# Gated cross-attention with a ternary feed-forward: 16-bit projections, halves made in place, another order on every engine

## The chip, the cores and the metric

The kernel runs on one NeuronCore of a Trainium2 chip. The metric is device time of one launch, in microseconds; of three runs of the kernel before the median is 1662.82 us (1661.55 to 1668.23). Engine names as the profile has them: PE (TensorE matmuls), PEld (its weight loads), DVE (VectorE), ACT (ScalarE), POOL (GpSimd), SP (SyncE, which here only starts transfers).

## The reference

All arithmetic is float32. `x` is 128 x 128 x 256 (batch, position, channel), `ctx` is 128 x 128 x 192, 16 heads of 16 channels.

```python
def attn(x, ctx, mask):                       # x is normalised first
    q = split_heads(x @ Wq); k = split_heads(ctx @ Wk); v = split_heads(ctx @ Wv)
    s = where(mask, q @ k.T * 16 ** -0.5, -max)
    return merge_heads(softmax(s) @ v) @ Wo
x = x + tanh(g_xattn) * attn(layernorm(x), ctx, mask)
h = gelu(layernorm(x) @ ternary(W1).T + b1)
x = x + tanh(g_ffn) * (h @ ternary(W2).T + b2)
```

`ternary` rounds a weight, divided by the mean of the weights' absolute values, to -1, 0 or 1.

## The kernel before, in words

The whole of `x` stays in SBUF (`xres`). Stage one is the attention. It goes through 64 groups of two batches; stage two, the feed-forward, goes through 32 steps of four batches and is hardly touched by the change. Each engine runs its own instruction list, written out by hand in Python; engines meet at semaphores only, and every engine runs its list strictly in order. In the loop a group `g` works on the scores of its own two batches and, at the same time, prepares the next three groups (`g1`, `g2`, `g3`).

A group has eight slots on PE, one per unit of four heads (`scores(pe, g, b, u, ...)`). A slot holds four exact score matmuls and four rough ones (`rough_head`), which give DVE the row maxima of a unit further on (`take_max`); then the weighing of an earlier unit (`weigh`), and one or two pieces of the preparation. These are: `transpose_x` and `transpose_ctx`, `project_q`, `project_k`, `project_v` in float32, `transpose_max` (the row maxima of a batch, rounded and split into two float16 parts by `round_max` and `low_max`), `transpose_attn` and `project_out`. All transposes and the output projection write the same PSUM bank, `tr_bank`; the q, k and v projections write `pj_bank`. Each PE function is given in `tr` who must have emptied `tr_bank` before it starts.

Numbers that must be exact in 16-bit matmuls are split into a high and a low half. For q and k, ACT copies PSUM to the float16 high half (`high_q`, `high_k`) and DVE subtracts (`low_q`, `low_k`). For the probabilities ACT writes the exponentials in float32 (`exponentials`); their upper 16 bits, read as bfloat16, are the high half, and POOL makes the low half in a tile of its own (`low_prob`, `probl`).

The halves of q and k reach the layout that the scores need by DMA (`move_heads`, eight transfers per batch, started by SP). The row maxima go the same way: PE transposes them, ACT copies them to `smaxT` (`copy_maxT`), and SP starts the transfer (`move_max`).

The layer norm before the attention is 14 small steps per group on DVE (`ln_part`, L672 to L697), spread one by one between the larger DVE instructions (`norm(i)`); three Newton steps give the root. ACT applies it (`apply_x`).

The functions that the change touches, with their lines, are these.

## Time and profile before

| | |
|---|---|
| median of three runs | 1662.82 us |
| profiled execution, its own time | 1664.17 us |
| span of its trace | 1662.4 us |
| mean granted TensorE clock | 0.984 |
| PE busy | 1508.0 us (91%) |
| DVE busy | 1489.1 us (90%) |
| ACT busy | 939.8 us (57%) |
| POOL busy | 668.8 us (40%) |

The span runs from the first to the last instruction; 1.8 us of the profiled execution lie around it. Busy times are of each engine alone and overlap each other. A matmul's duration in the trace includes the time until its last result is out, so that consecutive matmuls overlap: the distance between two starts says what one costs, the duration says when a reader can begin. The same holds in a smaller way for DVE and ACT. The attention stage takes about the first 1130 us, the feed-forward the rest.

### The profile page before, as it was taken

How to read it: one execution, taken by the hardware profiler on the slowest of the kernel's cores; microseconds unless marked ns; L12 is line 12 of the kernel's file. 1: busy time of each engine (PE TensorE's matmuls, PEld its weight loads, DVE VectorE, ACT ScalarE, POOL GpSimd, SP SyncE). 2: the span in 40 equal slices, each digit the busy share in tenths (PEclk: the TensorE clock that was granted, in tenths of full speed). 3: DMA queues.
4: the chain of work that ended last, by engine and by line, in shares of the span. 5: the costliest groups of instructions: out<-in, count | busy, mean ns of one | idle time of the engine just before them, and what ended most of it. 6: DMA issues, size and time to landing. Idle time of an engine off the chain costs nothing.

```text
span 1662.4 us, 48262 instructions
## 1 busy us (share of the span) xinstructions
PE 1508.0 (91%) x14501; PEld 1007.7 (61%) x14501; DVE 1489.1 (90%) x4379; ACT 939.8 (57%) x1799; POOL 668.8 (40%) x813
## 2 busy tenths in 40 slices
PE   3899999999999999999999999987999999999998
PEld 2566666666666666666666666655666666666665
DVE  7799999999999999999999999987888888888886
ACT  2456666665656666565656566654555555555554
POOL 5354555455555545554555545552111111111111
PEclk9899999999999999999999999996999999999999
DMA  2333333333333333333333333321010110101101
GB/s 78 92 99 85 96 84 88 93 86 97 84 96 83 97 84 94 86 87 95 86 97 83 98 83 95 81 49 55 26 38 25 38 38 25 38 25 38 38 25 51
DMA packets 207471, 117.93 MB, mean 71 GB/s; under 512 B 24912, under 2 KB 207184, under 8 KB 207440
## 3 DMA queue, kind: packets, MB, share of 16 engines
q1 hardware_dynamic: 207440, 117.54, 26.2%
q8 instruction: 17, 0.28, 0.1%
q14 instruction: 14, 0.11, 0.0%
HBM read 32.53 MB, written 16.78 MB: 30 GB/s over the span
## 4 chain that ended last, share of the span: by engine, by line
PE 55%; DVE 26%; issue 13%; ACT 3%; DVEq 2%; ACTq 0%; DMA 0%
PE bank L1069 12%; PE bank L312 9%; PE bank L1098 5%; PE bank L1099 5%; DVE smax L751 5%; PE bank L336 5%; PE bank L319 4%; PE bank L303 4%; DVE rstd L691 3%; DVE xres L796 3%; DVE k L721 3%; PE bank L392 2%; DVE rstd L693 2%; DVE y L1056 2%; DVE rstd L684 2%
## 5 line engine op out<-in xcount | busy, mean ns | idle before, releaser
L924 POOL TENSOR_TENSOR probl<-prob 128x512 f16<-128x512 f32 x512 | 529.2, 1042 | 531.2 <-ACT prob L602 530.3
L602 ACT ACTIVATE prob<-bank,masks 128x512 f32<-128x512 f32 x512 | 345.4, 688 | 138.9 <-PE bank L371 138.9
L751 DVE TENSOR_REDUCE smax<-bank 128x4 f32<-128x512 f32 x512 | 348.2, 681 | 13.5 <-PE bank L336 9.7
L1085 DVE TENSOR_TENSOR hidl<-hid 128x512 f16<-128x512 f32 x256 | 226.0, 883 | 80.5 <-ACT hid L1080 79.7
L1080 ACT ACTIVATE hid<-bank,b_sb 128x512 f32<-128x512 f32 x256 | 176.1, 688 | 211.3 <-PE bank L1069 205.3
L1069 PE MATMUL bank<-y,w1T 128*128 128x512 f16 x1024 | 264.6, 381 | 29.2 <-DVE y L1056 28.0
L1163 POOL TENSOR_TENSOR xres<-xres,b2g 128x1024 f32 (+1 forms) x32 | 75.7, 2366 | 431.4 <-ACT yln L1033 413.5
L1098 PE MATMUL bank<-w2T,hid 128*128 128x256 f16 x1024 | 237.4, 273 | 0.6 <-ACT w2T L1013 0.6
L1099 PE MATMUL bank<-w2T,hidl 128*128 128x256 f16 x1024 | 237.4, 273 | 0.0
L336 PE MATMUL bank<-k_rows,q_rows 64*128 64x128 f16 x2048 | 226.8, 220 | 5.6 <-DMA q_rows<-smaxT 3.4
L371 PE MATMUL bank<-q_rows,k_rows 64*128 64x128 f16 x2048 | 201.7, 219 | 0.8 <-DMA q_rows<-smaxT 0.8
L392 PE MATMUL bank<-v,prob 128*128 128x48 f16 x2048 | 179.4, 187 | 0.7 <-POOL probl L924 0.7
L336 PEld LDWEIGHTS bank<-k_rows,q_rows 64*128 64x128 f16 x2048 | 121.7, 94 | 84.8 <-issue 63.2
L393 PE MATMUL bank<-v,probl 128*128 128x48 f16 x2048 | 172.3, 184 | 0.0
L312 PE MATMUL bank<-ctxT,wk_sb 128*128 128x256 f32 (+1 forms) x512 | 165.2, 430 | 0.9 <-ACT ctxT L553 0.8
L319 PE MATMUL bank<-wv_sb,ctxT 128*128 128x256 f32 (+1 forms) x512 | 163.4, 418 | 0.9 <-DVE k L721 0.9
L1069 PEld LDWEIGHTS bank<-y,w1T 128*128 128x128 f16 x1024 | 97.9, 98 | 104.2 <-issue 35.1
L392 PEld LDWEIGHTS bank<-v,prob 128*128 128x128 bf16 x2048 | 125.4, 97 | 55.0 <-issue 1.8
L303 PE MATMUL bank<-xlnT,wq_sb 128*128 128x256 f32 x512 | 142.2, 402 | 9.7 <-DVE v L742 8.9
L371 PEld LDWEIGHTS bank<-q_rows,k_rows 64*128 64x128 f16 x2048 | 129.3, 95 | 30.0 <-DMA q_rows<-smaxT 1.2
L411 PE MATMUL bank<-wo_sb,attnT 128*128 128x256 f32 x512 | 145.4, 407 | 1.1 <-ACT attnT L610 1.1
L393 PEld LDWEIGHTS bank<-v,probl 128*128 128x128 f16 x2048 | 130.0, 97 | 0.3 <-issue 0.3
(92 smaller groups left out, 2555.7 us busy)
## 6 DMA issues: line engine op xcount, KB each, us to landing
q_rows<-q SPq DMA_DIRECT2D x512, 64.0 KB, 2.5
k_rows<-k SPq DMA_DIRECT2D x512, 64.0 KB, 2.5
xres<-in_x_dram SPq DMA_DIRECT2D x64, 256.0 KB, 2.7
out_dram<-ystage SPq DMA_DIRECT2D x32, 512.0 KB, 2.9
ctx_sb<-in_ctx_dram SPq DMA_DIRECT2D x64, 192.0 KB, 3.2
q_rows<-smaxT SPq DMA_DIRECT2D x128, 8.0 KB
w_raw<-in_L_ffn_W_dram SPq DMA_DIRECT2D x2, 1024.0 KB, 7.0
prob<-in_L_xattn_Wq_dram SPq DMA_DIRECT2D x1, 256.0 KB, 4.2
```

The source lines that it names most:

```text
L312: last = pe.matmul(pj_bank[:, m * T:(m + 1) * T], wk_sb[0:rows, k, m * P:(m + 1) * P], ctxT[g.parity][0:rows, k, :], start=(k == 0), stop= ...
L319: last = pe.matmul(pj_bank[:, b * D:(b + 1) * D], ctxT[g.parity][0:rows, k, b * S:(b + 1) * S], wv_sb[0:rows, k, :], start=(k == 0), stop= ...
L336: return pe.matmul(sm_bank[u % 2][:, c * S:(c + 1) * S], q_rows[g.parity][RB:RB + RK, b, u * UH + c, :], k_rows[g.parity][RB:RB + RK, b, u ...
L371: last = pe.matmul(st_bank[u % 2][:, c * S:(c + 1) * S], k_rows[g.parity][0:SK, b, u * UH + c, :], q_rows[g.parity][0:SK, b, u * UH + c, : ...
L392: pe.matmul(o, high, v, start=True, stop=False)
L393: last = pe.matmul(o, probl[u][:, c * S:(c + 1) * S], v, start=False, stop=True)
L602: act.activation(prob[u][:], st_bank[u % 2][:], ACT.Exp, bias=0.0, scale=masks[g.parity][:, 2 + b:3 + b]).then_inc(exp_done, 1)
L751: dve.tensor_reduce(smax[:, b, u * UH:(u + 1) * UH], sm_bank[u % 2][:].rearrange("p (h j) -> p h j", h=UH), AX.X, ALU.max).then_inc(max_ta ...
L924: pool.tensor_tensor(probl[u][:], prob[u][:], prob[u][:].bitcast(BF16)[:, 1::2], ALU.subtract).then_inc(prob_split, 1)
L1069: last = pe.matmul(h_bank[f % 2][:], w1T[:, k, f * P:(f + 1) * P], y16[g.parity][:, part, k, :], start=(i == 0), stop=(i == 2 * KD - 1))
L1098: pe.matmul(o, high, w2T[:, f, :], start=(f == 0 and b % 2 == 0), stop=False, skip_group_check=True)
L1099: last = pe.matmul(o, hidl[f % HBUF][:, b * S:(b + 1) * S], w2T[:, f, :], start=False, stop=(f == FB - 1), skip_group_check=True)
```

## The change

Every projection of the attention stage becomes three float16 or bfloat16 matmuls (high by high, high by low, low by high) instead of one in float32. The weights are scaled by 64 and split once at the start, on ACT and DVE. The normalised `x`, the context and the exponentials are split in place by POOL: the low half overwrites the lower 16 bits of each float32 (`low_x`, `low_ctx`, `low_prob`); both halves are transposed as 16-bit data, and ACT copies both (1024 columns instead of 512). The attention result is split after its transpose, by ACT and, new, by DVE (`low_attn`). The context is now cut 96 + 96 rather than 128 + 64.

The layer norm is made for four batches at a time, in every second group: DVE does the statistics and a first guess (`seed_x`), POOL the Newton steps (`root_x`, 14 small instructions). The sums of the weighing are kept in PSUM until they are normalised. The transfer of the row maxima is started by ACT, right behind its own copy. `k16` gets a second buffer. The rough scores run one unit further ahead. The lists of all five engines are reordered.

The core of the diff (without the startup's loads, the buffers' declarations and the last groups):

```diff
-            pe.wait_ge(ln_done, 2 * (g.n + 1))
-            for k in range(KD):
-                for b in range(2):
-                    last = pe.transpose(tr_bank[:, k * T + b * S:k * T + (b + 1) * S],
-                                        xln[:, b, k * P:(k + 1) * P], ident[:])
+            pe.wait_ge(x_split, g.n + 1)
+            for part in range(2):
+                for k in range(KD):
+                    for b in range(2):
+                        o = ((part * KD + k) * 2 + b) * S
+                        last = pe.transpose(tr_bank[:].bitcast(F16)[:, o:o + S],
+                                            halves(xln[:, b, k * P:(k + 1) * P], part), ident16[:])
             last.then_inc(x_transposed, 1)
...
+        SPLIT = ((0, 0), (0, 1), (1, 0))
+        def by_batch(m):
+            return pj_bank[:].rearrange("p (b m s) -> p m b s", m=KD, b=2)[:, m]
+        def typed(x, part):
...
         def project_q(pe, g, m):
             if m == 0:
                 pe.wait_ge(xT_copied, g.n + 1)
             for k in range(KD):
-                last = pe.matmul(pj_bank[:, m * T:(m + 1) * T], wq_sb[:, k, m * P:(m + 1) * P],
-                                 xlnT[:, k, :], start=(k == 0), stop=(k == KD - 1))
+                for i, (wp, xp) in enumerate(SPLIT):
+                    last = pe.matmul(by_batch(m), wq16[:, wp, k, m * P:(m + 1) * P],
+                                     typed(xT16[:, xp, k, :], xp).rearrange("p (b s) -> p b s", b=2),
+                                     start=(k == 0 and i == 0 and m == 0), stop=(k == KD - 1 and i == 2),
+                                     skip_group_check=True)
             if m == KD - 1:
                 last.then_inc(q_made, 1)
...
-                pe.wait_ge(norm_read, n * 2 + (half - 1))
+                pe.wait_ge(norm_done, n * 2 + (half - 1))
...
+                low = prob[u][:].bitcast(F16)[:, 2 * c * S:2 * (c + 1) * S:2]
                 pe.matmul(o, high, v, start=True, stop=False)
-                last = pe.matmul(o, probl[u][:, c * S:(c + 1) * S], v, start=False, stop=True)
+                last = pe.matmul(o, low, v, start=False, stop=True)
...
-            pe.wait_ge(attnT_copied, n + 1)
+            pe.wait_ge(attnT_split, n + 1)
             for k in range(KD):
-                last = pe.matmul(tr_bank[:, 0:D], attnT[:, k, :], wo_sb[:, k, :], start=(k == 0),
-                                 stop=(k == KD - 1))
+                for i, (wp, xp) in enumerate(SPLIT):
+                    last = pe.matmul(tr_bank[:, 0:D], attnT16[:, xp, k, :], wo16[:, wp, k, :],
+                                     start=(k == 0 and i == 0), stop=(k == KD - 1 and i == 2))
             last.then_inc(projected, 1)
             return [(x1_done, n + 1)]
...
-            scores(pe, g, 0, 0, (g, 1, 2))
+            tr = [(maxT_copied, 1)] if first else [(attnT_split, g.batch(0) - 1)]
+            scores(pe, g, 0, 0, (g, 1, 3))
             if not first:
                 weigh(pe, before, 1, 2)
-                tr = project_out(pe, g.batch(0) - 2, tr)
-            scores(pe, g, 0, 1, (g, 1, 3))
+            if left >= 2:
+                pe.wait_ge(v_split, g.n + 1)
+                project_q(pe, g2, 0)
+            scores(pe, g, 0, 1, (g1, 0, 0) if left >= 1 else None)
             if not first:
                 weigh(pe, before, 1, 3)
+            tr = transpose_max(pe, g, 1, tr)
             if left >= 2:
-                pe.wait_ge(v_split, g.n + 1)
-                project_q(pe, g2, 0)
+                project_q(pe, g2, 1)
                 tr = transpose_ctx(pe, g2, tr)
-                project_q(pe, g2, 1)
-            scores(pe, g, 0, 2, (g1, 0, 0) if left >= 1 else None)
+            scores(pe, g, 0, 2, (g1, 0, 1) if left >= 1 else None)
             weigh(pe, g, 0, 0)
-            tr = transpose_max(pe, g, 1, tr)
-            scores(pe, g, 0, 3, (g1, 0, 1) if left >= 1 else None)
+            if not first:
+                tr = project_out(pe, g.batch(0) - 2, tr)
+            scores(pe, g, 0, 3, (g1, 0, 2) if left >= 1 else None)
             weigh(pe, g, 0, 1)
-            if not first:
-                tr = transpose_attn(pe, g.batch(0) - 1, 1, tr)
             if left >= 2:
                 pe.wait_ge(q_split, g.n + 3)
                 project_k(pe, g2, 0)
                 project_k(pe, g2, 1)
-            scores(pe, g, 1, 0, (g1, 0, 2) if left >= 1 else None)
+            scores(pe, g, 1, 0, (g1, 0, 3) if left >= 1 else None)
             weigh(pe, g, 0, 2)
             if not first:
-                tr = project_out(pe, g.batch(0) - 1, tr)
...
+                tr = transpose_attn(pe, g.batch(0) - 1, 1, tr)
+            scores(pe, g, 1, 1, (g1, 1, 0) if left >= 1 else None)
             weigh(pe, g, 0, 3)
+            if left >= 1:
+                if left >= 2:
+                    pe.wait_ge(k_split, g.n + 3)
+                project_v(pe, g1, 0)
...
                 tr = transpose_x(pe, g.after(3), tr)
-            scores(pe, g, 1, 2, (g1, 1, 0) if left >= 1 else None)
+            scores(pe, g, 1, 2, (g1, 1, 1) if left >= 1 else None)
             weigh(pe, g, 1, 0)
             if left >= 1:
                 tr = transpose_max(pe, g1, 0, tr)
-                if left >= 2:
-                    pe.wait_ge(k_split, g.n + 3)
...
+                project_v(pe, g1, 1)
+            if not first:
+                tr = project_out(pe, g.batch(0) - 1, tr)
+            scores(pe, g, 1, 3, (g1, 1, 2) if left >= 1 else None)
             weigh(pe, g, 1, 1)
             tr = transpose_attn(pe, g.batch(0), 0, tr)
...
             act.copy(smaxT[b][:],
                      tr_bank[0:2 * HEADS, 0:S // 2].bitcast(F16)).then_inc(maxT_copied, 1)
+            act.wait_ge(maxT_copied, n + 1)
+            act.dma_start(q_rows[g.parity][HR:SR, b], smaxT[b][:]).then_inc(max_moved[b], 16)
...
             exponentials(act, g, 0, 0)
             exponentials(act, g, 0, 1)
+            copy_maxT(act, g, 1)
             if left >= 2:
+                high_q(act, g2)
                 copy_ctxT(act, g2)
-                high_q(act, g2)
-            copy_maxT(act, g, 1)
             exponentials(act, g, 0, 2)
             exponentials(act, g, 0, 3)
-            if not first:
-                copy_attnT(act, g.batch(0) - 1)
-            if left >= 3:
-                apply_x(act, g3)
             if left >= 2:
                 high_k(act, g2)
             exponentials(act, g, 1, 0)
+            if not first:
+                copy_attnT(act, g.batch(0) - 1)
             exponentials(act, g, 1, 1)
             if left >= 3:
                 copy_xT(act, g3)
             exponentials(act, g, 1, 2)
             if left >= 1:
                 copy_maxT(act, g1, 0)
+                high_v(act, g1)
             exponentials(act, g, 1, 3)
             copy_attnT(act, g.batch(0))
-            if left >= 1:
-                high_v(act, g1)
+            if left >= 4:
+                apply_x(act, g4)
...
+        def seed_x(dve, half, i):
+            past = half - 2
+            if i == 0:
+                dve.wait_ge(x_in, 16 * (half + 1))
+                for b in range(QB):
+                    last = dve.bn_stats(stats[:, b, :], row_of(half * QB + b))
+            elif i == 1:
+                if not (isinstance(half, int) and half == 2):
...
+        def low_x(pool, g):
+            pool.wait_ge(ln_done, 2 * (g.n + 1))
+            x = xln[:].rearrange("p b d -> p (b d)")
+            pool.tensor_tensor(x.bitcast(F16)[:, 0::2], x, x.bitcast(BF16)[:, 1::2], ALU.subtract).then_inc(x_split, 1)
+        def low_ctx(pool, g):
+            pool.wait_ge(ctx_loaded[g.parity], 16 * (g.half + 1))
+            x = ctx_sb[g.parity][:].rearrange("p b c -> p (b c)")
+            pool.tensor_tensor(x.bitcast(F16)[:, 0::2], x, x.bitcast(BF16)[:, 1::2], ALU.subtract).then_inc(ctx_split, 1)
...
+        def low_attn(dve, n):
+            dve.wait_ge(attnT_high, n + 1)
+            dve.tensor_tensor(attnT16[:, 1].rearrange("p k t -> p (k t)"), tr_bank[:, 0:KD * S],
+                              attnT16[:, 0].rearrange("p k t -> p (k t)"), ALU.subtract).then_inc(attnT_split, 1)
...
         def low_q(dve, g):
             dve.wait_ge(q_high, g.n + 1)
-            for b in range(2):
-                last = dve.tensor_tensor(q16[g.parity][:, 1, b], by_batch(pj_bank)[:, b], q16[g.parity][:, 0, b],
-                                         ALU.subtract)
-            last.then_inc(q_split, 1)
+            dve.scalar_tensor_tensor(q16[g.parity][:, 1].rearrange("p b m s -> p (b m s)"), pj_bank[:], 1.0 / WS,
+                                     q16[g.parity][:, 0].rearrange("p b m s -> p (b m s)"), ALU.mult,
+                                     ALU.subtract).then_inc(q_split, 1)
...
+            dve.tensor_reduce(sums_of(half), pv[:, :, 0:2 * HD].rearrange("p h (two d) -> p h d two", two=2), AX.X,
+                              ALU.add).then_inc(sums_taken, 1)
+        def sums_of(half):
+            return pv_bank[half][:, HB * VC:HB * (VC + HD)].rearrange("p (h d) -> p h d", h=HB)
...
-            dve.tensor_tensor(attn[b][:, heads, :], attn[b][:, heads, :],
+            dve.wait_ge(sums_taken, n * 2 + (half + 1))
+            if not (isinstance(n, int) and n < 2):
+                dve.wait_ge(attn_transposed, n - 1)
+            dve.tensor_tensor(attn[b][:, heads, :], sums_of(half),
```

POOL's list of a group is now this; the startup's list has the same calls, with the memsets of the score tiles between them:

```diff
         def pool_group(pool, g, left):
             for b in range(2):
                 for u in range(UNITS):
                     low_prob(pool, g, b, u)
-                    if b == 1 and u == 0 and left >= 1:
+                    k = b * UNITS + u
+                    if g.parity == 1 and left >= 6 and k >= 4:
+                        for i in range(2 * k - 8, 2 * k - 6):
+                            root_x(pool, g.half + 3, i)
+                    if g.parity == 0 and left >= 4 and k < 3:
+                        for i in range(2 * k + 8, 2 * k + 10):
+                            root_x(pool, g.half + 2, i)
+                    if k == 3 and left >= 3:
+                        low_x(pool, g.after(3))
+                    if k == 4 and left >= 1:
                         pick_masks(pool, g.after(1))
+                    if k == 6 and left >= 3:
+                        low_ctx(pool, g.after(3))
```

How the change moves instructions is shown at two places of the loop. DVE, around the rounding and the splitting of the row maxima, in a group that also carries norm work. Before (`smax` the row maxima, `stats` and `rstd` the layer norm, `attn` the weighed sums):

```order
L759 TENSOR_SCALAR smax<-smax 128x16 [waits max_taken]
L672 REGISTER_ALU
L691 TENSOR_TENSOR rstd<-rstd 128x2 [waits ln_step]
L766 SCALAR_TENSOR_TENSOR smax<-smax 128x16 [waits max_rounded]
L775 ISA
L780 RECIPROCAL rsum<-bank 128x8 [waits attn_transposed,weighed]
```

Now, the same place, in the second group of each pair:

```order
L896 TENSOR_SCALAR smax<-smax 128x16 [waits max_taken]
L770 ISA
L772 ISA [waits x_in]
L772 BN_STATS stats<-xres 128x6
L772 ISA
L772 BN_STATS stats<-xres 128x6
L772 ISA
L772 BN_STATS stats<-xres 128x6
L772 ISA
L772 BN_STATS stats<-xres 128x6
L903 SCALAR_TENSOR_TENSOR smax<-smax 128x16 [waits max_rounded]
L832 TENSOR_TENSOR attnT<-bank,attnT 128x256 [waits attnT_high]
```

Between the rounding and the splitting there is one small step before, and four statistics of a row of `x` now; behind it the new low half of the attention result.

ACT, around its copy of the row maxima of the second batch. Before (`prob` the exponentials):

```order
L593 COPY smaxT<-bank 32x128 [waits max_moved1]
L598 REGISTER_ALU
L601 REGISTER_ALU [waits scored]
L602 ACTIVATE prob<-bank,masks 128x512 [waits weighed]
L598 REGISTER_ALU
L602 ACTIVATE prob<-bank,masks 128x512 [waits weighed,scored]
```

Now:

```order
L631 COPY smaxT<-bank 32x128 [waits max_moved1]
L635 DMA q_rows<-smaxT 2x16x128 [waits maxT_copied]
L596 ISA
L600 ISA [waits q_made]
L601 ACTIVATE q_0<-bank 128x512 [waits q_moved1,q_moved0]
L592 COPY ctxT_0<-bank 96x1024 [waits v_made,ctx_transposed]
L639 REGISTER_ALU
L642 REGISTER_ALU [waits scored]
L643 ACTIVATE prob<-bank,masks 128x512 [waits weighed]
```

The copy is followed by the start of the transfer, then by the high half of q and the copy of the transposed context, both of which stood ahead of it before; the third exponential comes behind all of them.

## Rows read from the trace of the kernel before

**Rows 1.** Windows, all engines: window, us, then busy us (count) of PE, PEld, DVE, ACT, POOL, PEclk, DMA share, GB/s

```profile
100.00:1100.00 1000.00, 926.97 (x10292) 614.24 (x10291) 951.97 (x2937) 607.11 (x1240) 527.85 (x711) 1.00 0.34 90
...
1200.00:1600.00 400.00, 376.99 (x2626) 257.01 (x2625) 333.16 (x917) 215.06 (x352) 59.17 (x25) 1.00 0.10 33
```

**Rows 2.** Timeline of DVE: start us, us, line, operation, tiles, [idle before <- releaser]

```profile
500.29 0.76 DVE L714 TENSOR_TENSOR q<-bank,q 128x256 f16<-128x256 f32 x2 [0.45 <-ACT q L565]
...
505.34 0.48 DVE L796 SCALAR_TENSOR_TENSOR xres<-bank,gates,xres 128x256 f32 x1
...
509.88 0.98 DVE L684 TENSOR_SCALAR rstd<-rstd 128x2 int32<-128x2 int32 x1
...
517.24 0.76 DVE L714 TENSOR_TENSOR q<-bank,q 128x256 f16<-128x256 f32 x2 [0.25 <-ACT q L565]
...
525.04 1.00 DVE L789 TENSOR_TENSOR attn<-attn,rsum 128x128 f32<-128x128 f32 x1
```

**Rows 3.** Timeline of POOL, same columns

```profile
509.79 1.04 POOL L924 TENSOR_TENSOR probl<-prob 128x512 f16<-128x512 f32 x1 [0.85 <-ACT prob L602]
...
523.83 2.06 POOL L924 TENSOR_TENSOR probl<-prob 128x512 f16<-128x512 f32 x2
```

**Rows 4.** Groups by line and form, 200 to 1000 us: busy us, mean ns | idle before

```profile
L751 DVE TENSOR_REDUCE smax<-bank 128x4 f32<-128x512 f32 x377 | 256.6, 681 | 6.3 <-PE bank L336 3.6
...
L336 PE MATMUL bank<-k_rows,q_rows 64*128 64x128 f16 x1515 | 167.5, 219 | 0.0
...
L691 DVE TENSOR_TENSOR rstd<-rstd 128x2 f32<-128x2 f32 x141 | 52.5, 372 | 0.0
...
L742 DVE SCALAR_TENSOR_TENSOR v<-bank,masks,v 128x256 f16<-128x256 f32 x94 | 41.2, 481 | 1.1
...
L675 DVE BATCH_NORM_STATS2 stats<-xres 128x6 f32 x96 | 36.2, 418 | 1.8
```

**Rows 5.** Timeline of PE in the attention stage

```profile
500.81 0.44 PE L401 MATMUL bank<-ident,attn 128*128 128x128 f32 x2
501.11 2.36 PE L312 MATMUL bank<-ctxT,wk_sb 128*128 128x256 f32 x7
...
505.10 0.23 PE L336 MATMUL bank<-k_rows,q_rows 64*128 64x128 f16 x1
...
505.43 0.20 PE L392 MATMUL bank<-v,prob 128*128 128x48 f16 x1
...
505.95 0.65 PE L282 MATMUL bank<-ident,xln 128*128 128x128 f32 x4 [0.15 <-DVE xres L796]
...
515.07 0.44 PE L292 MATMUL bank<-ident,ctx_sb 128*128 128x128 f32 x2 [0.70 <-DVE xres L796]
...
515.56 1.03 PE L303 MATMUL bank<-xlnT,wq_sb 128*128 128x256 f32 x4
```

**Rows 6.** Timeline of PE in the feed-forward

```profile
1300.70 0.27 PE L1098 MATMUL bank<-w2T,hid 128*128 128x256 f16 x1
1300.81 0.27 PE L1099 MATMUL bank<-w2T,hidl 128*128 128x256 f16 x1
```

**Rows 7.** Timeline of ACT

```profile
500.59 1.27 ACT L602 ACTIVATE prob<-bank,masks 128x512 f32<-128x512 f32 x2
...
502.56 1.10 ACT L537 ACTIVATE xln<-xres,rstd 128x256 f32 x2 [0.44 <-DVE rstd L687]
...
506.64 0.59 ACT L545 COPY xlnT<-bank 128x512 f32<-128x512 f32 x1 [0.31 <-PE bank L282]
...
507.71 0.24 ACT L593 COPY smaxT<-bank 32x128 f16<-32x128 f16 x1
...
511.01 0.85 ACT L582 ACTIVATE v<-bank,masks 128x256 f16<-128x256 f32 x2 [0.82 <-PE bank L319]
```

**Rows 8.** Timeline of the queue of SP

```profile
500.70 0.67 SPq L230 DMA_DIRECT2D q_rows<-smaxT  x1
```

**Rows 9.** Windows, PE alone: window, us, busy us (count), PEclk, DMA share, GB/s

```profile
1122.00:1128.00 6.00, 4.66 (x32) 0.50 0.49 155
```

484 lines of the change are left out of this document (293 added, 191 removed).

## The prediction

> **What bounds the kernel now.** I read the busy time by stretch first. From 100 to 1100 us DVE is busy 952.0 us of 1000 and PE 927.0, at the full granted clock of 1.00, ACT 607.1 and POOL 527.9 [rows 1]. Then the timeline of DVE: the low half of q comes at 500.29 and again at 517.24 us, so one group lasts 16.95 us [rows 2], and DVE works 0.952 x 16.95 = 16.1 us of it. The reader is to see that DVE is the bound and that PE, ACT and POOL wait for it. In the feed-forward two 256-column float16 matmuls start 0.11 us apart, PE is busy 377.0 of 400 us [rows 1, 6]; its lists are the same but for one wait, and I leave it at its time.
>
> Part of the 16.1 us is not work. A step of 128 x 2 numbers took 0.98 us from 509.88 on, and POOL's 1.04 us instruction ran from 509.79 to 510.83; a normalisation took 1.00 us at 525.04, until 526.04, while POOL ran until 525.89 [rows 2, 3]. So an instruction of DVE on SBUF alone waits until POOL's own ends. The Trainium skill ("SBUF — State Buffer", "Who interferes with whom") says the same of a DVE instruction with two SBUF inputs, or in a two-port mode, beside one of POOL that reads SBUF, and that one with a PSUM input stays free. These rows bear out the lock.
>
> Last I looked at who holds `tr_bank`. The transpose of the context waited 0.70 us for DVE's addition [rows 5]. PE, ACT and DVE hand this bank to each other, and this chain, not the load, is what I follow below.
>
> **PE.** Per group the four float32 projections are 32 recorded passes. Four take 1.03 us with 0.17 of tail, 0.215 each, so 6.9 us at best; seven of k take 2.36 [rows 5], at which rate it is up to 10. Now 48 passes of 256 columns at 0.11 us [rows 6] make 5.3. PE loses 1.6 to 4 us of work a group; I take 3. Sixteen 16-bit transposes stand for eight float32 ones: four cost 0.65 with tail [rows 5]; eight half as dear each come to the same. Price 0, bounds -0.5 and +0.7.
>
> **DVE.** In two groups 28 norm steps become one set: eight statistics become one group's four plus small steps. One of the 14 kinds, L691, took 52.5 us in the 47 groups between 200 and 1000 us, three per group, 0.37 each [rows 4]. Twelve small steps at 0.37, or half of it where the mean is mostly lock, give 2.2 to 4.4 us, less some 0.5 that stays. The two new low halves of the attention result cost 0.35 each, half of 0.76 [rows 2]. The low halves of q and k are one instruction instead of two, 0.66 or so against 0.76. The normalisation reads PSUM and so no longer waits for POOL; the weighing that reuses the bank now waits for it instead of for the sums, 0.3 us later, and comes a slot later: 0, or 0.3 if DVE is late. In sum DVE's need goes from 16.1 to between 13 and 15.2.
>
> **POOL** gains per group a split of 512 columns (1.04 by rows 3), one of 384 (0.8), and seven Newton steps at 0.2 to 0.3: 8.9 becomes about 12. It is not the bound, but the lock is now taken most of the time.
>
> **ACT.** Copying 512 columns from PSUM took 0.59 us, 0.48 to the next one; 256 columns more cost about 0.21, so 1024 cost 1.0, 0.92 to the next. That adds 0.7 a group. New are two starts of a transfer. On SP this start held the queue for 0.67 us [rows 8]. The trace shows none on ACT: the bounds are 0 (it hides in ACT's idle time) and 1.34 (it must let one start of SP go first); I take 0.66, the row. ACT must first wait for its own copy, and behind the start are queued, in the second batch's place, the high half of q, the context's copy and the third exponential (the second listing of ACT's order); PE waits for the first two with its k and output projections. SP loses two starts a group and its wait for ACT. Nothing is gained on PE by the earlier transfer: its rough and exact scores have 0.0 of idle time [rows 4]. The Trainium skill ("Perfetto Trace Analysis", "DMA Instruction — HWDGE") says that the sequencer is free only at the end of the reported time, which speaks against this edit; by the lower bound the sum below would be 0.7 us a group less.
>
> **The chain of a group**, from the end of the attention transpose that closes the group before. Durations are from rows 2, 4, 5 and 7; where two engines meet I use the duration, else the distance of starts.
>
> ACT: result seen 0.15, high half to 0.4, `apply_x` 1.1 to 1.5, two exponentials 1.2 to 2.7, `copy_maxT` to 2.95, start of its transfer 0.66 to 3.6, high q 0.6 to 4.2, context 1.0 to 5.2. PE: output projection 0.66 to 5.9, scores and weighing 0.6, k projection 1.32 to 7.8. ACT: high k to 8.7. DVE: low k 0.6, a row maximum 0.6 to 9.9, rounding and splitting with a wait for POOL (between 0.4 and 2; POOL is then at its backlog, 0.95) to 10.85, low half of the attention result to 11.25. PE: transposes of x to 11.85. ACT: copy to 12.75, exponential to 13.35, `copy_maxT` to 13.6, transfer 14.3, high v 0.86 to 15.15. DVE: low v 0.8, addition 0.45 to 16.4. PE: attention transpose to 16.8.
>
> So a group of even number takes 16.8 us, against 16.95: ACT has the greater part of the chain, and what PE and DVE save lies beside it. PE stalls four times in it, 4.5 us in sum.
>
> In the odd groups four statistics stand between the rounding and the splitting of the maxima (the second listing of DVE's order). They cost 4 x 0.34 (0.418 by rows 4, overlapping) = 1.35 us. The split is then ready near 2.6 us, when POOL has just begun on the first exponential (seen at 2.25), and waits until 3.3. Behind it on DVE stands the low half of the attention result, for which `tr_bank` and so the transpose of the maxima, the second half of q, the context and the output projection wait. The high half of q begins at 5.05 instead of 3.6: +1.4 us, and nothing after it has slack. An odd group takes 18.2 us.
>
> **Sum.** Thirty even groups: 30 x (16.8 - 16.95) = -4.5. Thirty odd ones: 30 x 1.25 = +37.5. Startup: ACT scales and rounds the weights in 12 instructions on the path of the first projection, nearest row 0.55 each [rows 7], 4 to 7 us, less the permuting copies of DVE; +3. End of the stage: two low halves on the last chain, +1. In sum +37, which I shade to +30, since a chain drawn from in-order lists leaves no overlap: 1664.2 + 30 = 1694 us. The profiled execution lies 1.4 us above the median of the three runs, so 1693. The bounds of the parts (start of a transfer, wait for POOL, order of the meeting points) are about 0.7 us a group either way: 1655 to 1735 for this case.
>
> **Rivals.** *The relief of DVE comes through.* If ACT's start costs nothing and the chain has more slack than I draw, DVE's need sets the group: 15.2 us, with the idle of before about 16. Gain 0.95 to 1.75 x 60 = 57 to 105: 1560 to 1607; half of it still gives 1635. For it: DVE is the bound of before, 16.1 of 16.95. Against it: 1.0 of lock per SBUF instruction, and POOL busy 12 of 16. It decides from the point where the chain of both groups is under 16.95. Chance 0.33.
>
> *The odd groups catch up.* The statistics fall into a time when DVE waits anyway, and both kinds of group take 16.9: 1660 to 1669. Chance 0.13.
>
> *PE's clock falls.* Between 1122 and 1128 us PE was busy 4.66 of 6 us and the granted clock was 0.50, 1.2 GHz; in the steady stage with 0.93 of busy time it was 1.00 [rows 1, 9]. The chain above leaves PE busy about 12.3 of 17.5 us. PE's share of the chain is near 4 us; at the lower clock for a third of the time it grows by 1.3 us: 1.3 x 60 = 80, 1745 to 1790. For it speaks the stretch at 1122; against it that PE there also stood idle in long pieces, while here the stalls are 1.5 us at most. It decides once the granted clock of the steady stage is below 1.00 for a tenth of the time. The Trainium skill ("TensorE: Matmul & The Clock Gate", "HAM oscillation — how this bites in real kernels") tells of kernels that fall to the half rate between bursts; whether this one does only the run can say. Chance 0.16.
>
> **How the numbers follow.** My forecast has 0.38. A difference of 0.5%, 8.3 us, is about what can be told from none. Faster by more: the first rival's 0.33 and a little of the forecast's lower end, 0.36. Within: 0.13. Slower by more: 0.51. The range leaves out the better half of the first rival and the worse half of the third: 1600 to 1765.
>
> **What would show it.** Right: DVE busy under 90% with waits for `q_high`, `k_high`, `v_high`; PE idle before L446, L297 and L383; ACT with a gap of 0.7 us behind each L631; L903 near 1 us in odd groups; odd groups longer by over 1 us than even ones. Wrong: groups of equal length under 16.5 us, or DVE still above 95%. If the granted clock is under 1.00 between 100 and 1000 us, the third rival holds. A start of a transfer that costs ACT nothing would take 0.7 x 60 = 40 us off my sum.

## The result, and the profile after

The changed kernel takes 1736.93 us (median of 4 runs, 1735.62 to 1738.82), the kernel before, run beside it, 1664.18 us: ratio 1.0436, 95% interval 1.0411 to 1.0461. It is slower by 73 us. The direction forecast was right, the size (+30) less than half of what came; the time lies within the range of 1600 to 1765. Times below are medians of a kernel's runs. They leave out two runs in a slower state of the chip, of 2725.85 us (ACT's start in the kernel before) and 2719.92 us (ACT's start later, statistics moved).

The two stretches of [rows 1], in the windows view of the kernel after (window, us, busy us of PE, PEld, DVE, ACT, POOL, granted clock, DMA share, GB/s; the second window is set later, since the attention stage now ends later):

```profile
100.00:1100.00 1000.00, 771.24 (x10899) 555.35 (x10898) 742.99 (x2097) 593.96 (x1101) 658.67 (x1149) 0.93 0.32 84
...
1260.00:1660.00 400.00, 377.31 (x2629) 257.23 (x2627) 332.72 (x913) 215.76 (x355) 58.93 (x25) 1.00 0.09 33
```

The feed-forward is as before. In the attention stage no engine is busy for 80% any more: DVE fell from 952 to 743, PE from 927 to 771, and POOL rose from 528 to 659. The engines have less to do and wait more for each other, and the granted clock is 0.93 where it was 1.00.

Cut into groups, from one low half of v on DVE (L879) to the next, the stage shows two causes. Windows of PE alone (us, busy us, granted clock, DMA share, GB/s) over three neighbouring groups:

```profile
215.34:234.37 19.03, 15.43 (x198) 0.82 0.31 79
234.37:251.59 17.22, 13.02 (x198) 1.00 0.35 95
251.59:269.86 18.27, 12.99 (x198) 1.00 0.30 78
```

The first of the three is an odd group at a fallen clock, the second an even and the third an odd one at the full clock. At the full clock an even group lasts 17.23 us and an odd one, which has the statistics, 18.26, nearly always to 0.02 us. In the kernel before, cut in the same way, they lasted 17.56 (even) and 16.34 (odd), mean 16.95. In 34 of the 56 middle groups the clock was below 1.00 for some time. Even groups then last 18.0 to 18.4 us and odd ones up to 19.2; odd ones that have only the end of a fall (0.97) are no longer than at the full clock. So a mean group went from 16.95 to 17.75 (+0.80) by the order of the work and on to 18.15 (+0.40) with the clock: over 56 groups 45 and 22 us. The rest is the startup, 1.8 us by the start of the third group, and some 3 us of the last groups and the stage's end.

Timeline of DVE in an odd group, which answers to [rows 2] (start us, us, line, operation, tiles, [idle before <- releaser]):

```profile
506.61 0.88 DVE L879 SCALAR_TENSOR_TENSOR v<-bank,masks,v 128x256 f16<-128x256 f32 x2 [2.48 <-ACT v L620]
507.40 0.47 DVE L937 SCALAR_TENSOR_TENSOR xres<-bank,gates,xres 128x256 f32 x1
...
509.53 0.17 DVE L896 TENSOR_SCALAR smax<-smax 128x16 f16<-128x16 f32 x1
509.79 1.41 DVE L772 BATCH_NORM_STATS2 stats<-xres 128x6 f32 x4
511.11 0.46 DVE L903 SCALAR_TENSOR_TENSOR smax<-smax 128x16 f16<-128x16 f32 x1
511.49 0.41 DVE L832 TENSOR_TENSOR attnT<-bank,attnT 128x256 f16<-128x256 f32 x1
```

The statistics (L772) sit between the rounding (L896) and the splitting (L903) of the maxima, and 3 us earlier the same engine had stood idle for 2.48 us. Timeline of PE and ACT, first in the same odd group, then in an even one at the full clock (they answer to [rows 5] and [rows 7]):

```profile
512.03 0.22 PE L383 MATMUL bank<-ident,smax 128*32 128x128 f16 x1 [1.66 <-DVE attnT L832]
512.29 0.26 ACT L631 COPY smaxT<-bank 32x128 f16<-32x128 f16 x1 [1.30 <-PE bank L383]
512.58 0.63 ACTq L635 DMA_DIRECT2D q_rows<-smaxT  x1
513.38 0.60 ACT L601 ACTIVATE q<-bank 128x512 f16<-128x512 f32 x1 [0.84 <-PE bank L328]
513.88 1.00 ACT L592 COPY ctxT<-bank 96x1024 f16<-96x1024 f16 x1
514.93 0.83 PE L446 MATMUL bank<-wo,attnT 128*128 128x256 f16 x6 [0.84 <-ACT ctxT L592]
...
563.37 0.43 PE L435 MATMUL bank<-ident,attn 128*128 128x128 f32 x2 [1.50 <-DVE xres L937]
567.66 0.60 ACT L601 ACTIVATE q<-bank 128x512 f16<-128x512 f32 x1 [0.92 <-PE bank L328]
570.52 1.47 PE L340 MATMUL bank<-ctxT,wk 96*128 96x256 bf16 x12
575.02 0.62 PE L297 MATMUL bank<-ident,xln 128*128 128x128 f16 x8 [0.79 <-DVE attnT L832]
577.44 0.63 ACTq L635 DMA_DIRECT2D q_rows<-smaxT  x1
580.60 0.43 PE L435 MATMUL bank<-ident,attn 128*128 128x128 f32 x2 [1.57 <-DVE xres L937]
```

The gap before L601 is put down to PE's L328, the second half of the q projection, but the start of the transfer in ACTq, which the view does not count as busy, ends last. In the odd group the start ends at 513.21 and L328 (0.83 us from 512.19 on) at 513.02; in the even one the start ends at 567.39 and L328 (from 566.18 on) at 567.01. So behind the start there is a second wait, 0.2 to 0.4 us shorter. Twelve k matmuls take 1.47 us where seven recorded float32 ones took 2.36. The waits between 200 and 1000 us, 44 groups (engine, line <- engine, tile, line: us in total, times, longest):

```profile
DVE v L879 <- ACT v L620: 103.8, 44, 2.5
...
PE bank L435 <- DVE xres L937: 59.4, 44, 1.6
...
DVE q L837 <- ACT q L601: 37.9, 44, 1.8
...
PE bank L297 <- DVE attnT L832: 35.2, 44, 0.8
...
PE bank L383 <- DVE attnT L832: 30.3, 22, 1.7
PE bank L446 <- ACT ctxT L592: 30.0, 37, 1.1
...
DVE k L843 <- ACT k L610: 26.1, 44, 0.6
```

DVE and PE wait for each other and for ACT in turn: this is a chain, as the prediction drew it. That it is not a load is what the experiments test.

### The profile page after: what moved, and what is told of

Read it like the earlier page. It is cut to its first block, busy times and chain, and to the rows that moved or that the text cites. A ratio compares the mean times of both kernels' runs of the same rounds, so it can differ in the third digit from the quotient of the medians.

```text
span 1734.1 us, 50733 instructions
## 1 busy us (share of the span) xinstructions
PE 1399.4 (81%) x16037; PEld 986.6 (57%) x16037; DVE 1321.3 (76%) x3637; ACT 975.8 (56%) x1747; POOL 860.2 (50%) x1363
## 3 DMA queue, kind: packets, MB, share of 16 engines
HBM read 32.53 MB, written 16.78 MB: 28 GB/s over the span
## 4 chain that ended last, share of the span: by engine, by line
PE 53%; DVE 19%; issue 12%; ACT 11%; ACTq 3%; DVEq 1%; POOL 0%; DMA 0%; POOLq 0%
PE bank L1235 11%; PE bank L369 7%; PE bank L1264 5%; PE bank L1265 5%; DVE smax L888 5%; PE bank L340 5%; PE bank L328 5%; ACT ctxT L592 4%; PE bank L446 3%; PE bank L426 2%; ACTq L635 2%; DVE attnT L832 2%; PE bank L297 2%; DVE y L1222 2%; ACT v L620 2%
## 5 line engine op out<-in xcount | busy, mean ns | idle before, releaser
L1075 POOL TENSOR_TENSOR prob<-prob 128x512 f16<-128x512 f32 x512 | 533.5, 1044 | 368.5 <-ACT prob L643 363.8
L369 PE MATMUL bank<-k_rows,q_rows 64*128 64x128 f16 x2048 | 213.2, 228 | 16.5 <-DVE smax L888 12.6
L404 PE MATMUL bank<-q_rows,k_rows 64*128 64x128 f16 x2048 | 214.5, 229 | 0.0
L426 PE MATMUL bank<-v,prob 128*128 128x48 f16 x2048 | 186.2, 191 | 0.8 <-POOL prob L1075 0.6
L427 PE MATMUL bank<-v,prob 128*128 128x48 f16 x2048 | 179.5, 187 | 0.0
L879 DVE SCALAR_TENSOR_TENSOR v<-bank,masks,v 128x256 f16<-128x256 f32 x128 | 56.2, 482 | 144.3 <-ACT v L620 144.3
L446 PE MATMUL bank<-wo,attnT 128*128 128x256 f16 x768 | 116.0, 291 | 48.3 <-ACT ctxT L592 43.6
L328 PE MATMUL bank<-xT,wq 128*128 128x256 bf16 (+1 forms) x768 | 133.8, 324 | 7.2 <-DVE wo L853 6.2
L427 PEld LDWEIGHTS bank<-v,prob 128*128 128x128 f16 x2048 | 136.5, 100 | 0.1
L1264 PEld LDWEIGHTS bank<-w2T,hid 128*128 128x128 bf16 x1024 | 100.2, 98 | 39.8 <-ACT w2T L1175 1.2
L585 ACT COPY xT<-bank 128x1024 f16<-128x1024 f16 x64 | 64.8, 1012 | 102.3 <-PE bank L297 102.3
```

The source lines that it names most:

```text
L328: last = pe.matmul(by_batch(m), wq16[:, wp, k, m * P:(m + 1) * P], typed(xT16[:, xp, k, :], xp).rearrange("p (b s) -> p b s", b=2), start= ...
L369: return pe.matmul(sm_bank[u % 2][:, c * S:(c + 1) * S], q_rows[g.parity][RB:RB + RK, b, u * UH + c, :], k_rows[g.parity][RB:RB + RK, b, u ...
L404: last = pe.matmul(st_bank[u % 2][:, c * S:(c + 1) * S], k_rows[g.parity][0:SK, b, u * UH + c, :], q_rows[g.parity][0:SK, b, u * UH + c, : ...
L426: pe.matmul(o, high, v, start=True, stop=False)
L427: last = pe.matmul(o, low, v, start=False, stop=True)
L1075: pool.tensor_tensor(prob[u][:].bitcast(F16)[:, 0::2], prob[u][:], prob[u][:].bitcast(BF16)[:, 1::2], ALU.subtract).then_inc(prob_split, 1)
```

## The experiments

All are edits of the changed kernel but one. "Even" and "odd" are group lengths at the full clock, read like the windows above; the changed kernel has 17.23 and 18.26. Ratios are to the kernel before, run beside each of them (medians 1664 to 1668 us), with a 95% interval; a difference of times between two experiments is uncertain by some 3 us for that reason. Group lengths and clock falls are those of one profiled execution of each kernel.

**The statistics alone.** They go to the place where DVE stood idle, one group earlier; SyncE starts their load ahead of the moves of q and k.

```diff
+                if g.parity == 0 and left >= 7:
+                    seed_x(dve, g.half + 3, 0)
                 low_v(dve, g1)
...
-                if g.parity == 1 and left >= 6 and i < SEED_PARTS:
+                if g.parity == 1 and left >= 6 and 0 < i < SEED_PARTS:
```

> The changed kernel with one part of it moved: the four bn_stats of the next pair's x (seed_x part 0, 1.41 us of VectorE in every second group) stand ahead of low_v in the even group, where VectorE waits 2.3 us for high_v, instead of between round_max and low_max in the odd group; SyncE starts that x load ahead of the q and k moves so that it is there in time. Theory (the time is a chain through ScalarE, TensorE and VectorE over tr_bank): the odd group, 18.26 us at full clock, loses about 1.0 to 1.4 us, 30 x 1.2 = 36 us, so about 1700 us, with L903 of the odd group near 0.3 us behind L896. Rival (VectorE's or GpSimd's load, or the 16-bit matmuls themselves, set the pace, and the place of 1.4 us on an engine that is busy 76% of the time is of no matter): within 5 us of 1737.

1671.29 us, ratio to before 1.0036 [1.0022, 1.0049]: 66 us less, where the theory had 36. Windows of PE, an odd and an even group, then DVE in a later odd group:

```profile
240.47:257.31 16.84, 13.02 (x198) 1.00 0.30 76
257.31:274.53 17.22, 13.01 (x198) 1.00 0.41 101
...
515.91 0.17 DVE L896 TENSOR_SCALAR smax<-smax 128x16 f16<-128x16 f32 x1
516.12 0.17 DVE L903 SCALAR_TENSOR_TENSOR smax<-smax 128x16 f16<-128x16 f32 x1
516.22 0.42 DVE L832 TENSOR_TENSOR attnT<-bank,attnT 128x256 f16<-128x256 f32 x1
```

From the start of L896 to the end of L832 it is now 0.73 us, where the odd group above had 2.37. The 1.64 us between them are nearly all the statistics (1.32 from their start to L903's) and 0.29 more of L903, its wait for POOL, which went with them. The odd group lost 1.42 of the 1.64 us; that this is nearly the 1.41 us for which the four statistics are busy is chance. The even group did not move. That is 30 groups x 1.42 = 43 us. Most of the other 23 go with the clock: it falls in 11 of the 56 middle groups instead of 34, and what its falls add to these groups went from 23 to 3 us. I had not said that the clock would come back with it.

**ACT's start alone, given back to SyncE.**

```diff
-            act.wait_ge(maxT_copied, n + 1)
-            act.dma_start(q_rows[g.parity][HR:SR, b], smaxT[b][:]).then_inc(max_moved[b], 16)
...
                 move_k(sp, g.after(1), 1, split1, scored_before)
+            move_max(sp, g, 1, max_b1)
...
+            if left >= 1:
+                move_max(sp, g.after(1), 0, max_b0)
```

> The changed kernel with the transfers of the row maxima begun by SyncE again, in the places they had in the kernel before; ScalarE no longer spends 0.63 us on each start. Theory (ScalarE's start stands on the chain twice in a group): 55 groups lose 0.6 to 1.2 us each, so 35 to 65 us, 1672 to 1702 us; TensorE's waits for attnT and ctxT shrink. Rival (the start is hidden behind ScalarE's idle time, which is 44%): no change, within 5 us of 1737. Third: the wait goes over to SyncE's queue, the scores of the second batch wait for max_moved, and it is slower than 1740.

1672.23 us, 1.0032 [1.0017, 1.0047], at the far end of the theory's range. Windows of PE, an odd and an even group, then ACT in an even group:

```profile
243.80:261.57 17.77, 12.99 (x203) 1.00 0.30 77
261.57:277.93 16.36, 13.01 (x204) 1.00 0.38 102
...
573.96 0.60 ACT L609 ACTIVATE q<-bank 128x512 f16<-128x512 f32 x1 [0.45 <-PE bank L336]
...
584.21 0.85 ACT L628 ACTIVATE v<-bank,masks 128x256 f16<-128x256 f32 x2 [0.50 <-PE bank L358]
```

Even 16.36 (-0.87), odd 17.77 (-0.49): 0.68 a group, 41 us over 60. Two starts last 1.25 us, so this is about half of them. The gaps say where the other half is: ACT's gap before the high half of q was 0.92 us with the start and is 0.45 without it, the one before v was 0.90 and is 0.50. These two differences make the 0.87 us. What is left of each gap is a wait for PE's projection (L336, L358), the second wait that the start had covered. The clock came back here too, in all but 2 of the 56 groups, and most of the remaining 24 us go with it.

**More work for PE, to hold the clock.** Matmuls that nothing needs, before four of PE's waits (abridged):

```diff
+                pe.matmul(spare, wq16[:, 1, 0, 0:P], wo16[...120 columns...], start=True, stop=True)  # x12 and x8
...
+                project_v(pe, g1, 0)
+                project_q(pe, g2, 0)
```

> The changed kernel with matmuls added that nothing needs, in four places of a group where TensorE waits for tr_bank: 8 and 12 matmuls of 120 columns into unused PSUM columns, and one project_q half and one project_v half computed twice. They add about 2.4 us of TensorE work to a group, nearly all of it inside waits of 0.5 to 1.7 us. Theory (the fall of the granted clock to 1.2 GHz costs 0.4 us a group, 24 us of the 73): the granted clock of 100 to 1000 us goes from 0.93 to 1.00, the groups come to 17.3 and 18.3, and the time is 1710 to 1725 us. Rival A (the clock has cost nothing, since TensorE waits anyway): clock 1.00 and within 5 us of 1737. Rival B (the added matmuls are on the chain): above 1745.

1774.02 us, 1.0655 [1.0625, 1.0685]: slower by 37 us, as rival B had it, and the clock still fell (0.97 between 100 and 1100, in 19 of the 56 groups). Windows of PE over three neighbouring groups:

```profile
237.37:256.93 19.56, 16.68 (x230) 0.91 0.33 90
256.93:275.49 18.56, 15.23 (x230) 1.00 0.28 70
275.49:293.56 18.07, 15.24 (x230) 1.00 0.35 93
```

At the full clock the groups grew by 0.84 and 0.30: part of what I had put into waits was on the chain. And a larger share of busy time did not hold the clock: PE was busy 15.2 us of 18.1 to 18.6 here, and the clock fell; with the statistics moved it was busy 13.0 us of 17.0, and the clock was 0.99 in the same stretch. The test failed as a way to price the clock, since it changed the chain too.

**ACT's start in the kernel before.** ACT starts the transfers there, SyncE does not.

```diff
             act.copy(smaxT[b][:],
                      tr_bank[0:2 * HEADS, 0:S // 2].bitcast(F16)).then_inc(maxT_copied, 1)
+            act.wait_ge(maxT_copied, n + 1)
+            act.dma_start(q_rows[g.parity][HR:SR, b], smaxT[b][:]).then_inc(max_moved[b], 16)
```

> The kernel before with one part of the change alone: ScalarE begins the transfers of the row maxima behind its copy, SyncE no longer does. Theory (a start takes ScalarE 0.63 us, and what it costs depends on whether ScalarE is on the chain; in the kernel before ScalarE waits most, and VectorE and TensorE set the pace): 0 to +20 us, 1662 to 1684. Rival (the earlier transfer is a gain of its own): 1640 to 1658. Rival (the start costs as much here as in the changed kernel): +35 us or more.

1667.50 us, 1.0021 [1.0001, 1.0041], within the theory's range. Timeline of ACT and its queue:

```profile
507.70 0.24 ACT L589 COPY smaxT<-bank 32x128 f16<-32x128 f16 x1
507.97 0.62 ACTq L593 DMA_DIRECT2D q_rows<-smaxT  x1
509.02 0.69 ACT L601 ACTIVATE prob<-bank,masks 128x512 f32<-128x512 f32 x1 [1.08 <-PE bank L367]
```

The same 0.62 us, and at most 0.4% of time: where DVE sets the pace, ACT has room for it; its next exponential waits for PE until 0.43 us after the end of the start. In the changed kernel, where ACT is on the chain, the same start costs 65 us, what goes with the clock included.

**Both moved.**

> The changed kernel with both parts moved: the four bn_stats ahead of low_v in the even group, and SyncE beginning the transfers of the row maxima. Alone the first gave groups of 16.84 and 17.22 us, the second 16.36 and 17.77. Theory (both stand on the same chain and are not the same wait): the second takes another 0.5 us off either group, 16.3 and 16.7, mean 16.5, so 60 x 0.53 = 32 us less than 1671, about 1640, and faster than the kernel before by some 25 us. Rival (they shorten the same wait, so the second gives nothing more; most of the 66 us was TensorE's clock, which comes back with either): 1665 to 1673.

1635.64 us, 0.9804 [0.9788, 0.9821], near the 1640 of the theory; even 16.36, odd 16.12 (the theory had 16.7 and 16.3). The two are separate waits of one chain. The clock fell again in 24 of the middle 56 groups.

**ACT's start later instead of on SyncE**, once with the statistics moved, and once alone:

```diff
                 high_q(act, g2)
                 copy_ctxT(act, g2)
+            start_max(act, g, 1)
...
                 high_v(act, g1)
+                start_max(act, g1, 0)
```

> The changed kernel with the four bn_stats moved as in the run above, and with ScalarE still beginning the transfers of the maxima, but one piece of its own work later: behind the copies of q and ctx (batch 1) and behind that of v (batch 0). Theory (what costs is that the start stands between the copy and what TensorE and VectorE wait for, not that ScalarE does it): most of what SyncE's start gives, 1640 to 1660. Rival (0.63 us of ScalarE are 0.63 us wherever they stand, or the transfer now comes too late for the scores): 1668 us or more.

> The changed kernel with one thing moved: ScalarE starts the transfers of the maxima behind the copies of q and ctx (batch 1) and behind that of v (batch 0); the statistics stay between round_max and low_max. With SyncE's start in its place the time was 1672. Theory (the place of the start costs, not that ScalarE does it): 1660 to 1680. Rival (what SyncE's start gave was ScalarE's 1.26 us of work a group): 1710 or more.

With the statistics moved 1628.45 us, 0.9768 [0.9748, 0.9787], even 16.36, odd 16.08: below the theory's range. It is 7 us less than with SyncE's start, though the groups are equal to 0.04 us; the clock fell in 11 groups instead of 24. Alone 1673.66, 1.0039 [1.0023, 1.0055], even 16.37, odd 17.73, the same as by SyncE to 0.04 us. Timeline of ACT and its queue, with the statistics moved:

```profile
612.42 0.60 ACT L601 ACTIVATE q<-bank 128x512 f16<-128x512 f32 x1 [0.45 <-PE bank L328]
612.73 0.62 ACTq L636 DMA_DIRECT2D q_rows<-smaxT  x1
612.92 1.00 ACT L592 COPY ctxT<-bank 96x1024 f16<-96x1024 f16 x1
```

The start still lasts 0.62 us, but it runs from 612.73 to 613.35 while ACT works on the copies of q and ctx, which stand ahead of it in the list. In the place that the change gave it, it must first wait for the copy of the maxima, and nothing of ACT's runs beside it. What costs is that place, ahead of the copies for which PE and DVE wait, not that ACT does it.

**More load on DVE in a place where it waits.** Four more bn_stats ahead of low_v in the odd group, with the statistics moved.

> The kernel with the four bn_stats moved ahead of low_v in the even group (1671 us), and four more bn_stats that nothing needs, at the same place of the odd group: 1.41 us of VectorE added to each second group, in its wait for high_v. Theory (VectorE's place decides, not its load): 1671 +/- 3 us. Rival (the load on VectorE, or what it shares with GpSimd, sets the pace): 1680 to 1710.

1670.61 us, 1.0021 [1.0009, 1.0034]: nothing lost for 1.41 us more in every second group, groups of 17.23 and 16.85 where they were 17.22 and 16.84. DVE's load does not set the pace.

**Without low_attn.** The low half of the attention result is left out (its buffer is zero); PE goes on behind ACT's copy.

> The changed kernel, statistics and starts where the change has them, without low_attn: the low half of attn^T is left out (its buffer is zero), TensorE multiplies as before and goes on behind ScalarE's copy. This prices the added VectorE step in the hold of tr_bank, twice in a group. Theory: each is 0.41 us and 0.1 to 0.3 us of VectorE's reaction on the chain, in both places: 0.9 us a group, 1680 us, and less if the clock comes back to 1.00 with it (1655). Rival (one of the two places is slack): 1700 to 1715. Rival (no place matters): 1732 or more.

**low_attn earlier.** The second one of a group ahead of the row maximum, its rounding and splitting, and nothing else:

```diff
+            if not first:
+                low_attn(dve, g.batch(0) - 1)
             if left >= 1:
                 take_max(dve, g1, 0, 3)
                 round_max(dve, g1, 0)
...
-            if not first:
-                low_attn(dve, g.batch(0) - 1)
```

> The changed kernel with one step moved on VectorE: the second low_attn of a group ahead of take_max, round_max and low_max. TensorE's wait for it (L297) is 0.8 us in each group. Theory (low_attn is late because of what VectorE does first): 0.4 to 0.8 us a group, 1690 to 1713 us, and another 24 us less if the clock goes to 1.00. Rival (the wait passes on to TensorE's next one, for the maxima or for x): 1730 or more.

Without it 1666.20 us, 0.9999 [0.9984, 1.0014]; earlier 1676.37, 1.0063 [1.0043, 1.0083]. Both are faster than the theories gave for a clock that does not come back (1680, and 1690 to 1713), and it did not: it falls in 35 and in 31 of the 56 middle groups. At the full clock the even group takes 16.27 us without the step and 16.26 with it earlier. So in the even group the 0.42 us of the step cost nothing, and its place cost 0.97, more than the 0.79 that PE's wait for it showed. Too few odd groups are at the full clock (4 and 2) to say the same of them. Timeline of the even group with the step earlier, DVE and PE:

```profile
238.11 0.69 DVE L843 SCALAR_TENSOR_TENSOR k<-bank,k 128x512 f16<-128x512 f32 x1 [0.61 <-ACT k L610]
238.95 0.42 DVE L832 TENSOR_TENSOR attnT<-bank,attnT 128x256 f16<-128x256 f32 x1
239.29 0.68 DVE L888 TENSOR_REDUCE smax<-bank 128x4 f32<-128x512 f32 x1
...
239.53 0.61 PE L297 MATMUL bank<-ident,xln 128*128 128x128 f16 x8
```

PE's L297 has no wait in front of it now, where it had 0.79. The falls of the clock, here mostly in odd groups, go with 0.37 us of a mean group: 17.15 us against 16.78 at the full clock.

**All of it, and add_attention ahead of low_v.**

```diff
+                if not first:
+                    add_attention(dve, g.batch(0) - 1)
                 low_v(dve, g1)
```

> The kernel with the statistics moved and ScalarE's start put later (1629 us; groups of 16.08 and 16.36), and two VectorE steps of the tr_bank chain taken earlier in its order: the second low_attn ahead of take_max, round_max and low_max, and the second add_attention ahead of low_v. TensorE's waits behind them are 0.79 and 1.17 us a group there. Theory (VectorE's order, not its load, holds the chain): each gives half to all of its wait, 0.6 to 1.6 us a group, so 1550 to 1595 us, limited by what comes late next. Rival (VectorE's 13.2 us in 16.2 and TensorE's 13.0 are near what the dependences allow, or the maxima and v that now come later hold TensorE instead): 1615 to 1635. Also possible: TensorE's clock falls more often, 1630 or more.

> The fastest version so far (1534 us: statistics moved, low_attn and add_attention earlier on VectorE, ScalarE's start behind q and ctx or v) with the starts of the maxima given to SyncE. Theory (a start costs where it stands ahead of a copy that others wait for; behind it ScalarE has room, 0.63 us in idle time): the same within 8 us, or up to 20 us slower, since SyncE starts 16 other transfers in a group of now 14.8 us and the maxima wait behind them. Rival (ScalarE's 1.26 us a group are on the chain even so): 1500 to 1520.

With ACT's late start 1534.10 us, 0.9209 [0.9190, 0.9228]; with SyncE's start 1531.31, 0.9172 [0.9155, 0.9189], the fastest kernel here, by about as much as its own runs differ (1528.57 to 1532.86). The first went past the theory's range (1550 to 1595), the second lies within its own. What add_attention gave apart from low_attn has no run of its own. Two groups of the first, and the stage (windows of PE, then of all engines, 100 to 1000 us, as in the first fence):

```profile
203.29:218.51 15.22, 12.95 (x201) 1.00 0.43 114
218.51:232.95 14.44, 12.75 (x198) 1.00 0.37 91
...
100.00:1000.00 900.00, 779.48 (x11953) 575.74 (x11948) 799.96 (x2293) 650.40 (x1202) 715.65 (x1236) 0.99 0.40 101
```

Groups of 14.44 and 15.22 us against the 16.95 of the kernel before: this is the relief of DVE that the change makes possible and did not bring. PE and DVE are now busy 87 and 89% of the stage. In the waits of this kernel between 200 and 900 us, DVE's for v is gone from the head of the list, and PE's for the addition (L941 here) is down to 14.8 us in 23 times:

```profile
POOL prob L1083 <- ACT prob L644: 114.0, 140, 1.6
ACT prob L644 <- PE bank L404: 44.3, 71, 0.7
...
PE bank L446 <- ACT ctxT L592: 30.2, 47, 0.6
```

## Why the prediction was right in direction and wrong in size

**Right.** The mechanism: a chain over `tr_bank` through ACT, PE and DVE sets the group, and the work saved lies beside it. DVE's busy time in a mean group is 0.743 x 18.15 = 13.5 us, within the 13 to 15.2 forecast; PE's is 13.0 (12.3). All three of DVE's waits for ACT and PE's idle time before L446, L297 and L383 are in the view. The odd group is 18.26 us for 18.2, and longer than the even one by 1.03. The statistics in their place cost 1.42 us for 1.35 to 1.4, by an edit of that part alone. Startup came to 1.8 us for 3. ACT's gap around each start is 0.84 to 0.92 us, longer than the start's 0.63. The Trainium skill ("Perfetto Trace Analysis", "DMA Instruction — HWDGE") has the sequencer free only at the end of the reported time; these gaps agree.

**Right by luck.** The prediction said that a start which costs nothing would take 0.7 x 60 = 40 us off its sum, and 41 us came at the full clock. But its chain has two starts of 0.66 in every group, so by the chain it should have said about 80. The 0.68 us a group come from something that it did not have: half of each start covers a wait for PE's q or v projection.

**Wrong, first term: the clock.** I kept it out of the sum as a rival of chance 0.16, by the argument that the idle stretches here are 1.5 us at most. They are 1.7 at most, and the clock still fell to 1.2 GHz in 34 of 56 groups, for 3 to 7 us at a time. So the argument failed, not the rival; but the rival's price of 1.3 us a group (80 us) failed too. It had the lower clock for a third of the time; measured is a seventh (a mean of 0.93), and 0.40 us a group, some 22 us. By the condition that I gave (a clock under 1.00 in the steady stage) the third rival came true beside the forecast, not in place of it: I had made them exclude each other, and a sum of chances over such cases has no place for both.

**Second term: the even group**, 17.23 us for 16.8, 13 us over 30 groups. Counted from the end of the attention transpose at 563.80, high q begins at 3.86 for 3.6; the k projection ends at 8.19 for 7.8; the transposes of x end at 11.84 for 11.85; v is rounded at 15.36 for 15.15; the next attention transpose ends at 17.23 for 16.8. The order of the steps holds, several sizes do not. Too small were the two starts, behind each of which ACT's next work begins 0.25 us later than drawn, the output projection (0.83 for 0.66) and the k projection (1.47 for 1.32), and the way from the addition to the end of the transpose (0.57 for 0.4). Too large were the high half of k (0.63 for 0.9) and the rounding and splitting with its wait for POOL (0.61 for 0.95). That the transposes of x end when forecast is two errors that cancel.

**Third: the shading** from +37 to +30. The groups came out longer than drawn, 17.23 for 16.8 and 18.26 for 18.2, so these 7 us went in the wrong direction. There is slack in the chain, the half of each start named above, but it shows when a step is taken out and does not shorten the chain as it stands.

Together, from +30: shading 7, even groups 13, odd groups 2, clock 22, startup -1, end of the stage 2. That makes 75, measured 73.

**Also wrong in detail.** L903 in odd groups was said to be near 1 us behind POOL; it took 0.46. So the wait for POOL was 0.3 us, where 0.7 had been drawn (2.6 to 3.3), and the statistics made most of the odd group's length.

**The rivals.** The relief of DVE did not come through, but its price was right in kind: with four moves of order and no less work the kernel goes to 1534, below the 1560 that I gave as its best. "The odd groups catch up" is refuted: they are 1.03 us longer than the even ones, and 1.42 us came back with the statistics moved.

**Open.** What makes the clock fall. It nearly held with either of the first two edits (11 and 2 of the 56 groups) and fell in 24 with both. It fell in 31 with low_attn earlier and in 35 without it, in none once everything was moved, and in one when SyncE made the starts there. Neither PE's share of busy time nor its longest idle stretch (1.6 to 1.7 us in the changed kernel and in the one with the statistics moved) puts these kernels in order. The 22 us are read from groups at both levels of one trace; no run changed the clock alone.

## What to carry to other kernels

When a change takes work from the busiest engine, draw the chain through the shared buffer before counting the relief: here four statistics and two starts of a transfer in the wrong place, and one low half behind the row maxima, ate all of it, and the same instructions in other places cost nothing that the groups show. Where an engine has a long wait in its list (2.5 us before low_v), move there whatever no other engine waits for, and put first what hands a shared bank on. Do not shade the sum of a chain drawn from in-order lists for slack: here it came out too short. But before you price the removal of a step, look for the wait that stands just behind it. A clock that may fall is a term to be added, not only a rival.

## What the runs showed of the hardware that was not expected

The granted clock fell in a pattern that repeats every six groups over most of the stage (lengths 19.03, 17.22, 18.27, 18.40, 18.27, 17.99, and again 19.05, 109 us after the first). It fell in the kernel with matmuls added (PE busy 82 to 84% of a full-clock group) and nearly held in one busy 76%. The Trainium skill ("TensorE: Matmul & The Clock Gate", "A second HAM failure mode: psum-queue depth-cycling") describes an engine that idles briefly between groups of matmuls and goes back and forth between the rates. The trace agrees: the clock goes back and forth with idle stretches of 1.7 us at most. What starts a fall it does not show.

The start of a transfer took ACT 0.62 to 0.65 us, and SyncE 0.67 for the same transfer ([rows 8]). Behind a wait for ACT's own copy it left a gap of 0.84 to 0.92 us in ACT's work; behind copies already under way (612.73 above) it ran beside them and left none. The Trainium skill ("DMA: Bandwidth & Descriptors", "Issuing engines are not separate DMA queues") says that starting on several engines saves only the sequencer's time; here no group became clearly shorter by ACT's start, even at its best place: 16.36 and 16.08 us against 16.36 and 16.12 with SyncE's, and 1534 against 1531 us in the fastest order.
